# Five stages' first operands loaded a stage ahead, and the memory stage's keys and substitution reordered

## The reference

```
q, k, v  = x @ Wq + bq, x @ Wk + bk, x @ Wv + bv           # 16 heads of 16
mod      = sigmoid(x @ cg_W + cg_b + (cons_vec @ am_W + am_b))
ctx      = softmax(q k^T / 4 * mod) v                      # modulated
causal   = mha(x,   ca_Win, ca_Wout)                       # 4 heads of 64
ctx      = ctx * 0.3 + causal * 0.7
meta     = mha(ctx, mc_Win, mc_Wout)                       # 4 heads of 64
ctx      = ctx * (1 - META_W) + meta * META_W
x        = layernorm(x + ctx @ Wo + bo)
...
k = (x @ Wk.T) by head;  k = k / max(norm(k), 1e-12)       # second layer
M = M - alpha * (M k_t) k_t^T + beta * v_t k_t^T           # token by token
```

## Time and profile before

| | us |
|---|---|
| median of 3 runs | 4131.39 |
| lowest, highest | 4127.64, 4134.43 |
| the profiled execution | 4137.06 |
| span of its trace | 4135.0 |

### The profile page before, as it was taken

One profiled execution on the slowest core, in us unless ns is written; L12 is line 12 of the kernel. 1 busy time (PEld: TensorE's weight loads), 2 busy tenths in 40 slices (PEclk: granted clock), 3 DMA queues, 4 the chain that ended last, 5 costly groups with the idle time before them and its releaser, 6 DMA issues. The chain is left out here.

```text
span 4135.0 us, 55466 instructions
## 1 busy us (share of the span) xinstructions
PE 3641.5 (88%) x19168; PEld 1696.5 (41%) x19168; DVE 2392.0 (58%) x3942; ACT 1488.9 (36%) x2186; POOL 1519.5 (37%) x1333
## 2 busy tenths in 40 slices
PE   8979999997999798999879646668898989999996
PEld 3412222222333242332545435533454565565653
DVE  5669999994666316665542356977786741111112
ACT  2227777774444323444213223311454211111112
POOL 0032222223777504777336403043652332222221
PEclk9979999998999899999979865789899999999998
DMA  5542222212110252110532331354443113333333
GB/s 170 187 93 65 77 60 66 76 40 60 39 44 26 73 184 73 44 42 11 169 108 85 124 127 45 115 123 103 136 138 105 41 40 113 86 108 94 104 99 92
DMA packets 314060, 370.70 MB, mean 90 GB/s; under 512 B 55217, under 2 KB 248001, under 8 KB 312833
## 3 DMA queue, kind: packets, MB, share of 16 engines
q1 hardware_dynamic: 274208, 304.31, 24.0%
q0 software_dynamic: 31776, 57.19, 5.8%
q10 hardware_dynamic: 7872, 6.56, 0.6%
HBM read 232.23 MB, written 127.30 MB: 87 GB/s over the span
## 5 line engine op out<-in xcount | busy, mean ns | idle before, releaser
L596 DVE TENSOR_REDUCE modulated_mx<-modulated_ring 128x1 f32<-128x512 f32 x1024 | 651.6, 683 | 51.9 <-PE modulated_ring L502 46.1
L580 ACT ACTIVATE modulated_probs<-modulated_scores 128x1024 f32<-128x1024 f32 x512 | 496.1, 1021 | 181.4 <-PE modulated_scores L523 181.4
L3191 DVE TENSOR_TENSOR expert_h<-expert_gelu,expert_bank 128x512 f32<-128x512 f32 x128 | 88.0, 688 | 389.8 <-PE expert_bank L3120 384.3
L532 PE MATMUL modulated_acc<-modulated_probs,modulated_v 128*32 128x512 f32 x2048 | 273.4, 606 | 0.6 <-ACT modulated_probs L580 0.6
L3162 ACT ACTIVATE expert_gelu<-expert_bank 128x512 f32<-128x512 f32 x128 | 76.4, 597 | 548.1 <-PE expert_bank L3120 545.3
L502 PE MATMUL modulated_ring<-modulated_k,modulated_q 64*128 64x512 bf16 x1024 | 239.5, 399 | 34.7 <-DMA modulated_v<-scratch_v 23.5
L523 PE MATMUL modulated_scores<-modulated_q,modulated_k 128*128 128x512 bf16 x1024 | 268.3, 384 | 0.8 <-ACT modulated_probs L580 0.2
L3080 POOL DMA_INDIRECT scratch_acc<-expert_y,expert_idx x64 | 101.0, 1577 | 427.4 <-DVE expert_y L3196 403.9
L996 POOL TENSOR_TENSOR meta_total<-meta_total,meta_probs 128x1024 f32<-128x1024 f32 x96 | 230.8, 2404 | 61.2 <-ACT meta_probs L905 59.4
L996 POOL TENSOR_TENSOR causal_total<-causal_total,causal_probs 128x1024 f32<-128x1024 f32 x96 | 230.9, 2405 | 61.0 <-ACT causal_probs L905 59.1
L927 DVE TENSOR_REDUCE causal_mx<-causal_maxima 128x2 f32<-128x1024 f32 x120 | 145.8, 1215 | 127.8 <-PE causal_maxima L795 127.8
(11 more groups left out here) (507 smaller groups left out, 7264.0 us busy)
## 6 DMA issues: line engine op xcount, KB each, us to landing
modulated_k<-scratch_k_part SPq DMA_DIRECT2D x192, 64.0 KB, 2.3
modulated_q<-scratch_q_part SPq DMA_DIRECT2D x180, 64.0 KB, 2.3
scratch_v<-proj_v SPq DMA_DIRECT2D x8, 1024.0 KB, 6.9
modulated_v<-scratch_v SPq DMA_DIRECT2D x16, 512.0 KB, 4.7
scratch_M<-steps_snap SPq DMA_DIRECT2D x16, 512.0 KB, 3.3
chunk_raw_v<-scratch_v SPq DMA_DIRECT2D x64, 128.0 KB, 2.9
chunk_mem<-scratch_M SPq DMA_DIRECT2D x32, 256.0 KB, 2.9
first_wg<-x_WgT SPq DMA_DIRECT2D x8, 1024.0 KB, 4.9
```

Of the source, the lines that this page charges most:

```text
L532: last = nc.tensor.matmul(acc[32 * j:32 * j + 32, :], vs[g % SLOTS][:, t, j, :], probs[u % NPROBS][j // 2][:, j % 2, :], start=(t == 0), s ...
L580: nc.scalar.activation(probs[u % NPROBS][i][:], sc[i][:], ACT.Exp, scale=SCALE).then_inc(s_exp, 1)
L596: V.tensor_reduce(mx[h % 2][:, x // 2, 1 - j % 2, j // 2, x % 2:x % 2 + 1], ring[bank_of["max", 4 * m + j]][:], AX.X, ALU.max).then_inc(s_ ...
```

## The change

**In front of each stage.** `hold_for_attention` sets buffers aside for the whole first attention, and the first operands of five stages go there during the stage in front. GpSimd, after its last `xT` load, loads the first group of `quad_attention` (25 transfers). `quad_attention` loads the first pair of `causal` on SyncE's queue before its last groups; `causal` loads the 8 weights and biases of `mix`; `mix` loads the first pair of `meta` before its last of 4 rounds, which is written out of the loop for it; `meta` loads the 6 weights and biases of `close`. Each waits for these loads at its end.

**At the start of the program** the 17 loads are parted in three, on three semaphores: 5 for `modps` and mod and 4 for q and k on SyncE's queue, 8 on ScalarE's. `mm.start` stands ahead of the wait.

```
-        weights = [(w["q"][:], rows(io["L0_attn_Wq"])), (w["k"][:], ...
+        weights = [[(am[:], io["am_W16"]), (cons[:], ...), (w["mod"][:], rows(io["cg_W16"])),
+                    (cgb[:], column(io["cg_b16"])), (amb[:], column(io["am_b16"]))],
+                   [(w["q"][:], rows(io["L0_attn_Wq"])), (bias["q"][:], ...), (w["k"][:], ...), (bias["k"][:], ...)],
+                   [(w["q2"][:], rows(ca)[:, :, 0:D]), ...
 
         @block.tensor
         def _(pe):
-            pe.wait_ge(s_w, 16 * len(weights))
+            mm.start(pe)
+            have(pe, 0)
...
-            mm.start(pe)
             with pe.Fori(0, NCH // 2) as i:
...
+                    if (j, kind, m) in ((0, "q", 0), (0, "q2", 0)):
+                        have(pe, 1 if kind == "q" else 2)
...
@@ GpSimd in project_hidden
                     loaded[j].done(pool.dma_start(xT[j][:], rows(io["hT"])[:, :, bass.ts(i * 2 + j, CH)]))
+            for x in (*PARTS, "v"):
+                stored[x].wait(pool, 1)
+            first = scr["heads16"]
+            load_heads(pool, first["q"], scr["q_part"], QUERY_PARTS, 0, s_heads)
+            load_heads(pool, first["k"], scr["k_part"], KEY_PARTS, 0, s_heads)
+            pool.dma_start(first["v"][:]...).then_inc(s_heads, 16)
+            pool.wait_ge(s_heads, 16 * 25)
...
@@ quad_attention
-            for g in range(SLOTS):
+            for g in range(1, SLOTS):
                 load(g)
...
+                if g + SLOTS == GROUPS:
+                    load_all(sp, ahead, s_ahead)
...
-            pe.wait_ge(s_made, 2)
             for m in range(AHEAD):
                 maxima(m, 0)
                 maxima(m, 1)
                 if m == KT + 1:
+                    pe.wait_ge(s_made, 2)
                     turn_shift(0)
...
@@ mix_and_project
+            with sp.Fori(0, B - 1) as i:
+                store(i)
...
+            load_all(sp, ahead, s_ahead)
+            store(B - 1)
+            sp.wait_ge(s_ahead, 16 * len(ahead))
...
@@ memory_projections
-            for c in range(QUADS):
-                jobs += [("k", g, c)] + [("kT", g, c - 1, m) for m in range(HH)] * (c > 0)
-            jobs += [("kT", g, QUADS - 1, m) for m in range(HH)]
+            for c in range(QUADS + 2):
+                jobs += [("k", g, c)] * (c < QUADS) + [("kT", g, c - 2, m) for m in range(HH)] * (c >= 2)
...
-                return [2 * (n % 2) + u for u in range(2)]
+                return [2 * (n % (3 if kind == "k" else 2)) + u for u in range(2)]
+            if kind == "kT":
+                return [6 + job[3]]
...
+        beside_keys = lambda c: ("share" if c % 2 == 0 else "rows", SUB - 1 - c // 2)
...
-            measure_and_make(1)
...
+            for c in range(QUADS + 1):
+                if c < QUADS:
+                    measure(1, c)
+                if c > 0:
+                    make_keys(1, c - 1)
+                if c == 0:
+                    laid_dots(0)
+                    act_s.wait(dve, ("kT", 0, QUADS - 1, HH - 1))
+                x, i = beside_keys(c)
+                substitute(x, 0, i)
+            for x, i in behind_keys:
+                substitute(x, 0, i)
+            laid_dots(1)
```

More of the change, by code:

```diff
@@ L280, in _ @@
         def _(sp):
-            load_all(sp, weights, s_w)
+            for n in range(2):
+                load_all(sp, weights[n], s_w[n])
             for s in stored.values():
@@ L349, in _ @@
         def _(dve):
-            dve.wait_ge(s_w, 16 * len(weights))
+            dve_s.start(dve)
+            have(dve, 0)
             dve.wait_ge(s_modps, KD)
@@ L748, in _ @@
         def _(sp):
-            for p in range(PAIRS):
+            for p in range(1, PAIRS):
                 s, r = p % SLOTS, slice(p * P, (p + 1) * P)
@@ L1041, in _, with store @@
         def _(sp):
-            load_all(sp, first_weights, s_first)
-            load_all(sp, weights, s_w)
             for s in stored.values():
                 s.start(sp)
-            with sp.Fori(0, B) as i:
+            def store(i):
                 for j in range(2):
@@ L1883, in memory_projections @@
         dve_names = []
+        halves_of = lambda x, g, i: [(x, g, i, part) for part in range(HALVES)]
+        beside_keys = lambda c: ("share" if c % 2 == 0 else "rows", SUB - 1 - c // 2)
+        behind_keys = [(x, i) for i in STEPS for x in ("share", "rows") if (x, i) not in [beside_keys(c) for c in range(QUADS + 1)]]
         for g in range(G):
```

238 lines of the change are left out of this document (122 added, 116 removed).

## The result

The changed kernel takes 4090.01 us (median of 4 runs, 4086.74 to 4096.48) against 4130.12 before (4 runs), a ratio of 0.9896 with a 95% interval of 0.9879 to 0.9912. Forecast were 4085.6 and 4072 to 4104. Run again later it gave 4094.42 against 4133.89, a ratio of 0.9908 (0.9893 to 0.9923). So the whole was right, a little too bright. Its parts were not all right: one half of the change was forecast too high and the other too low, and the experiments found one of the edits to work against the rest.

A forecast was written before the change was run, and what follows sets the result against it. The prediction took the kernel as a chain of stages, each bound by whichever wait ends last at its start. Gains of 10.0 + 8.8 + 8.2 + 3.2 + 1.4 + 10.1 + 4.1 = 45.8 gave 4085.6 us, range 4072 to 4104.

The forecast's parts named there:

- Start, 10.0: Program start: the first matmul comes at 8 us instead of 17.96, winning 10.0 us (range 8 to 12).
- it doesn't start early: Rival, 5%: competing sets of start loads land the input no sooner; costs 10 us, time 4100 to around no change.
- Second stage, 8.8: Second stage: first real scores at 259.2 instead of 268.03, now waiting for GpSimd's constants and shifts; 8.8 us won.
- rival of late loads: Rival, 6% (slower 3%): GpSimd's 25 issues cost far more beside VectorE's casts in the first stage; 4113 us.
- Pair stages, 8.2: Causal and meta: TensorE waits for VectorE's last constants instead of a load, 4.1 us won in each, 8.2 together.
- Mixing, 3.2: Mixing stage: without the weights beside it, plain lands in 4 to 4.6 us; 3.2 won (bounds 1 and 3.7).
- Closing, 1.4: Closing stage: only meta is awaited, landing after 2.7 to 4.6 us; TensorE starts at 1984.0 instead of 1985.42.
- First group's keys, 10.1: Memory stage: TensorE's waits before transposes shrink, so the first group's laid is complete at 2455.3, not 2465.43.
- Second group, 0.7 + 3.4: Memory stage: keys end 0.7 us sooner; the second substitution wins at most 3.4, then bound by SyncE's layout issues.
- queued keys: Rival, 10%: the second group's key chunks queue behind long substitution halves, so layouts begin 16.3 us later; 4102 us.
- The sum: Whole kernel: all terms together win 45.8 us, giving 4085.6 us from the median of 4131.39.
- The likeliest case: Whole kernel: the forecast itself, 4085.6 us, held at 70%, with its own range of 4077 to 4095.

The follow-up runs named there:

- start_act_waits: Changed kernel, but ScalarE issues its eight start loads only after the first set of five has landed; first matmul of mod at 9.99 us, against 13.95.
- all_mended: Changed kernel with small loads first, ScalarE's loads held back, earlier shifts, TensorE waiting for causal alone in mixing, 32 layouts on GpSimd; 4067.16 us, ratio 0.9843 to the kernel before.
- shift_first: Changed kernel, but in quad_attention GpSimd places the first shifts before the third slot's constants; that stage took 742.7 us instead of 749.1.
- mix_one_wait: Changed kernel, but in mixing TensorE waits for the causal chunk alone and VectorE for plain; the stage took 133.87 us instead of 136.34.
- mproj_only: Kernel before, with only the changed memory_projections (banks, key order, substitution between the second group's keys); 4112.69 us against 4132.35, ratio 0.995.
- close_meta_first: Changed kernel, but in meta_output SyncE issues the first two chunks' other five loads only after the first meta landed; the stage took 96.3 us instead of 94.2.
- keys_unmixed: Changed kernel, but the first group's substitution stands wholly behind the second group's keys again; the memory stage took 248.8 us instead of 257.1.
- layouts_pool: Changed kernel, but GpSimd issues 32 of the second group's 128 layouts, leaving SyncE 64 instead of 96; the memory stage took 244.3 us, 12.8 less.

## Why the prediction was right or wrong

**Start, 10.0: the step that failed.** "It lands after 2.7 to 4.6 us" took both ends from a start in which one queue was loading. The price of three queues that load at once was put on the input alone ("shares the engines now with three queues' loads, so 5.8 to 10"), and not on the five loads that `modps` waits for, though they share the same engines. The trace shows 3.1 MB moved in the first 12.5 us, at 248 GB/s and a share of 0.84, and `amb` was among the last. The rival "it doesn't start early", which names this, was priced at 10 lost; 6 were. start_act_waits (9.99) and all_mended (8.08) show the cause.

**Second stage, 8.8: right** to 0.1, with its new wait (VectorE's pause of 7.22 us forecast as 7), and shift_first shows the cause. The cover of the 25 loads was larger than reckoned: issued by 176.6 at 0.55 each, and the last, `heads_v`, landed after 5.9 us, at 181.4 where 191 was reckoned. The rival of late loads is out: 24 issues of 0.54 to 0.57 us and one of 1.08 in a stretch where VectorE casts, and 32 of 0.516 beside its multiplications. The rule of the Trainium skill, "SBUF — State Buffer", section "A bandwidth-pool intuition that's wrong (but worth ruling out)", by which such a transfer takes 3.1 us beside a VectorE copy, is borne out by no row here. Only the 25 stand beside casts, of 0.43 us each; a long copy was not tried.

**Pair stages, 8.2: right**, 4.2 and 4.1 within the stages; the other 0.6 of the table's 4.7 came at mixing's end.

**Mixing, 3.2: a third too much.** `plain` landed 5.4 us after its issue and not 4 to 4.6; four loads of 512 KB were then in flight, not two. mix_one_wait shows that 1.5 us of TensorE's wait were `plain` behind `causal`. **Closing, 1.4: too much.** TensorE's start won 0.8, since `meta` landed after 4.2. The stage as a whole won 2.4 against the trace of before, but most of that is scatter: from SyncE's first issue to TensorE's last matmul it takes 93.85 us before, 91.96 in mproj_only with the same code but without the slow stretch, and 91.50 in the changed kernel. Against mproj_only the edit wins 0.5. close_meta_first puts 3.7 of the 4.2 on the load itself, so this load was slower than the 2.7 that I took as its lower bound. The fit of the Trainium skill, "DMA: Bandwidth & Descriptors", section "Anatomy of one DMA", gives an estimate of 3.2 for 512 KB, but the page measured it on GpSimd's queue and this load is on SyncE's; here it was 3.7 alone and 4.2 with others behind it.

**First group's keys, 10.1: right**, 10.5.

**Second group, 0.7 + 3.4: the sum right, the reading wrong.** 5.6 were won. The wait for the layouts came as forecast (12.6 us for 13), and so did SyncE's 0.70 an issue. But I took the keys' gain of 0.7 as given and wrote of queued keys only as a rival that costs time against before. That rival was in fact at work: 11.3 of the 13.1 us that the new banks and order give were eaten by it. I set the kernel against the one before and not against the same kernel without the edit, so a loss inside a gain was not seen. It also made my theory for keys_unmixed wrong by 11 us and in sign.

**The sum.** 45.8 against 42.8 in the traces without chunk_attention's 5.6, and 40.1 in the medians. In that pair of traces the start's 6.0 too much, mixing's 1.0 and what was given back within the stages (2.1) stand against 1.5 more in the second group, 0.4 in the first, 1.6 in closing and meta, and 2.2 ahead of the first key matmul. Much of the second list is scatter: the closing stage's share is the clock, as above, and the way from TensorE's last in closing to the first key matmul, which no edit touches, took 350.1 us in the changed kernel's trace and up to 355.2 in the other thirteen (352.3 before). The medians say it more plainly. The stages in front gave 20.7 of a forecast 31.6, and the memory stage 19.7 of a forecast 14.2. The one was 10.9 too high and the other 5.5 too low, so that the sum came as near as it did is in part luck. The likeliest case's own range, 4077 to 4095, held.

## What to carry to other kernels

Price a load at the start by the bytes of all queues that are loading, not by its own size: while the engines are full, order within one queue only chooses which operand is late, and a set that is wanted later should be held back until the first has landed. In the closing stage, where only 0.5 us of the delay was the bytes behind, this brought nothing. When work is moved ahead of a wait, ask first what the engine's other customers start with: a gain in front of a wait is worth nothing if the thing waited for begins later by as much. Compare each edit with the kernel that has all the others, not only with the kernel before. And before a term of 1 or 2 us is booked, look at the same stage in a second trace of unchanged code, and at TensorE's granted clock in both.

## What the runs showed of the hardware

In the memory stage the multiplications of GpSimd and the two-operand work of VectorE in SBUF slow each other. From the changed kernel's timeline, VectorE's `rows` for the same size, first beside GpSimd's multiplications and then, in the second substitution, with GpSimd idle; and GpSimd's multiplication beside VectorE's copies out of PSUM and beside its substitution:

```profile
2514.61 5.37 DVE L2109 TENSOR_TENSOR mproj_k<-mproj_k,mproj_own 128x1664 f32<-128x1664 f32 x2
...
2608.93 3.68 DVE L2109 TENSOR_TENSOR mproj_k<-mproj_k,mproj_own 128x1664 f32<-128x1664 f32 x2
...
2463.54 1.04 POOL L1958 TENSOR_TENSOR mproj_masked<-mproj_laid,mproj_share_of 128x512 f32<-128x512 f32 x1 [1.25 <-PE mproj_bank L1994]
...
2535.05 2.17 POOL L1958 TENSOR_TENSOR mproj_masked<-mproj_laid,mproj_share_of 128x512 f32<-128x512 f32 x1 [1.74 <-PE mproj_bank L1994]
```

The same 128x1664 half pair takes 3.68 or 5.37 us, and the multiplication 1.04 or 2.17. Two multiplications fall on the slow pair, so each costs VectorE some 0.84 us. This is why the first substitution lasts 81.6 us in keys_unmixed (2500.93 to 2582.56) where the second takes 68.2: 16 multiplications of GpSimd lie beside the first, and 16 times 0.84 is 13.4. GpSimd's DMA issues did not do this: with 32 of them added, VectorE's first substitution took 65.9 us from the last key on in layouts_pool, and 65.7 in the changed kernel. And TensorE's clock moved stages without any edit: chunk_attention by 5.6 us, the closing stage by 1.9, the first matmuls of mixing by 1.6. Most terms of this prediction are no larger, so a gain is to be read stage by stage and from more than one trace.
